# Two engines share the making of sample-wise mixing matrices, with a new order around samples 2, 3 and the last ones

## The reference

```python
# conv step: groups = 4, K = 9, pad = 4
out = conv(x, weight) + (c @ c_weight.T)[:, :, None] + bias[None, :, None]
x = x + out
# mix step
h = gelu(embedding @ W0 + b0); h = gelu(h @ W1 + b1)
att = softmax(h @ W2 + b2)                        # 64 x 8
agg_w = einsum('bk,koi->boi', att, weight)        # one 128x128 matrix per sample
agg_b = att @ bias_k
x = x + einsum('boi,bih->boh', agg_w, x) + agg_b[:, :, None]
```

## Time and profile before

| what | value |
|---|---|
| runs | median 726.98 us of 3, 726.56 to 728.69 |
| the profiled execution | 725.75 us, with a span of 723.6 us from its first to its last instruction |
| busy share of the span | PE 99%, PEld 86%, ACT 83%, POOL 76%, DVE 64% |
| granted TensorE clock | 0.999 of full speed |
| DMA | 177.56 MB, mean 245 GB/s |

### The profile page before, as it was taken

The page is one execution under the profiler, slowest core; times in us unless marked ns, Lnnn a source line. Parts: engine busy times, 40 slices in busy tenths (PEclk is TensorE's granted clock), DMA queues, the critical chain, the costliest instruction groups (busy, mean ns, idle before and its releaser), DMA issues.

```text
span 723.6 us, 29229 instructions
## 1 busy us (share of the span) xinstructions
PE 713.3 (99%) x12419; PEld 622.5 (86%) x12419; DVE 465.5 (64%) x413; ACT 598.6 (83%) x456; POOL 546.6 (76%) x592
## 2 busy tenths in 40 slices
PE   8999999999999999999999999999999999999996
PEld 6899998998888888888888888888888888888885
DVE  6987667577777666566566566566566566576543
ACT  5988887888888888888888888888888888888843
POOL 2899999999999999866766766766766766767740
PEclk9999999999999999999999999999999999999999
DMA  6445867867876867887787778678768777777546
GB/s 225 158 151 183 285 229 241 286 201 268 283 248 230 293 237 254 281 271 255 249 291 258 241 262 287 225 250 275 268 225 294 245 249 269 243 249 270 191 156 239
DMA packets 66551, 177.56 MB, mean 245 GB/s; under 512 B 7437, under 2 KB 50008, under 8 KB 50264
## 3 DMA queue, kind: packets, MB, share of 16 engines
q1 hardware_dynamic: 66002, 176.93, 71.4%
q10 hardware_dynamic: 518, 0.17, 0.1%
HBM read 101.57 MB, written 75.50 MB: 245 GB/s over the span
## 4 chain that ended last, share of the span: by engine, by line
PE 82%; POOL 11%; DMA 4%; issue 1%; SPq 1%; DVE 0%; ACT 0%; DVEq 0%; POOLq 0%; ACTq 0%
PE ps L432 61%; PE ps L463 21%; POOL mix_prod L755 4%; POOL mix_prod L750 4%; DMA mix_dram<-mix_parts 2%; POOL mix_sum_f L758 2%; DMA mix_rep<-mix_dram 1%; DMA x_in<-in_x_dram 1%; POOL mix_f L762 1%; SPq L291 1%; POOL mix_parts L768 1%; POOL mix_parts L765 0%; ACT x_hi L515 0%; POOL par L745 0%; POOL par L774 0%
## 5 line engine op out<-in xcount | busy, mean ns | idle before, releaser
L432 PE MATMUL ps<-x_hi,cw_hi 32*128 32x512 f32 x3072 | 384.8, 385 | 0.9 <-ACT x_hi L515 0.6
L432 PE MATMUL ps<-x_hi,cw_lo 32*128 32x512 f32 x3072 | 384.1, 384 | 0.0
L511 ACT ACTIVATE x_ph<-x_in 128x2560 f32<-128x2560 f32 x63 | 318.6, 5058 | 2.7 <-DMA x_in<-in_x_dram 2.1
L613 DVE TENSOR_TENSOR y_lo<-ps,y_hi 128x512 fp32r<-128x512 f32 x256 | 159.2, 684 | 239.1 <-ACT y_hi L524 239.1
L432 PE MATMUL ps<-x_lo,cw_hi 32*128 32x512 f32 x3072 | 274.7, 385 | 0.0
L432 PEld LDWEIGHTS ps<-x_lo,cw_hi 32*128 32x128 f32 x3072 | 222.1, 183 | 21.1 <-issue 0.8
L463 PE MATMUL ps<-y_hi,mix_rep 32*128 32x512 f32 x2048 | 214.4, 385 | 1.6 <-DMA mix_rep<-mix_dram 1.6
L432 PEld LDWEIGHTS ps<-x_hi,cw_hi 32*128 32x128 f32 x3072 | 195.3, 183 | 22.6 <-issue 1.7
L432 PEld LDWEIGHTS ps<-x_hi,cw_lo 32*128 32x128 f32 x3072 | 194.8, 183 | 20.3 <-issue 0.2
L537 ACT ACTIVATE z_out<-ps,par 128x1024 f32<-128x1024 f32 x124 | 146.1, 1236 | 75.3 <-PE ps L463 75.3
L602 DVE TENSOR_TENSOR x_lo<-x_ph,x_hi 128x2560 fp32r<-128x2560 f32 x63 | 189.4, 3007 | 2.2
(11 more groups left out here) (80 smaller groups left out, 92.7 us busy)
## 6 DMA issues: line engine op xcount, KB each, us to landing
x_in<-in_x_dram SPq DMA_DIRECT2D x64, 1024.0 KB, 7.3
out_dram<-z_out SPq DMA_DIRECT2D x63, 1024.0 KB, 5.0
mix_rep<-mix_dram SPq DMA_DIRECT2D x256, 128.0 KB, 2.6
mix_dram<-mix_parts SPq DMA_DIRECT2D x64, 128.0 KB, 7.0
out_dram<-x_in SPq DMA_DIRECT2D x2, 512.0 KB, 3.5
z_out<-in_L_cond_weight_dram SPq DMA_DIRECT2D x1, 512.0 KB, 3.9
cw_nat<-in_L_cond_weight_dram SPq DMA_DIRECT2D x1, 144.0 KB, 2.2
w_sb<-in_L_cond_W_dram ACTq DMA_DIRECT2D x2, 64.0 KB, 5.1
```

The lines of the kernel that those rows point to most:

```text
L432: mm = pe.matmul(y_at(s)[:, g, :], w[rows, m, :], x_at(xx[buf(s)], rows, m), start=i == 0, stop=i == CONV - 1)
L511: nc.scalar.activation(x_ph[buf(s)][:, :, :, :], by_lane(x_in[buf(s)]), ACT.Copy).then_inc(x_split_ph, 1)
L613: nc.vector.tensor_tensor(y_lo[s[1]][:, g, :], y_at(s)[:, g, :], y_hi[s[1]][:, g, :].bitcast(F32), ALU.subtract).then_inc(y_lo_made, 1)
```

## The change

GpSimd makes the matrices of the first three samples (`FIRST = 3`) with the same instructions as before, outside any loop. VectorE makes all others, at the end of its slot: a copy of the weights, eight terms that are summed in two chains (`mix_even`, `mix_odd`; the identity is added with the first odd term), and three instructions for the two halves. In the slot before the last, VectorE makes two matrices, those of samples 62 and 63.

In slot 2, VectorE takes y(2)'s rests ahead of x(3)'s. SP's order differs in the last slots. In DRAM a matrix lies as 32 rows of 4 KB (a row holds the four groups' two halves) where it lay as 128 rows of 1 KB.

```diff
+FIRST = 3
...
-        mix_dram = [nc.dram_tensor(f"mix_dram{k}", [P, 2, P], F32, kind="Internal").ap() for k in range(2)]
+        mix_dram = [nc.dram_tensor(f"mix_dram{k}", [Q, G, 2, P], F32, kind="Internal").ap() for k in range(2)]
...
+        def by_pool(s):
+
+            return isinstance(s[0], int) and number(s) < FIRST
...
-                sp.dma_start(mix_dram[b][:, :, :], mix_parts[b][:, :, :].bitcast(F32)).then_inc(mix_stored[b], DMA)
+                sp.dma_start(mix_dram[b].rearrange("c g h o -> g c (h o)"),
+                             mix_parts[b].rearrange("p h o -> p (h o)").bitcast(F32)).then_inc(mix_stored[b], DMA)
...
-                    sp.dma_start(rep_at(s)[Q * r:Q * r + Q, :, :, :].bitcast(F32).rearrange("c g h o -> c g (h o)"),
-                                 mix_dram[b].rearrange("(g c) h o -> c g (h o)", g=G)).then_inc(mix_loaded[b], DMA)
+                    sp.dma_start(rep_at(s)[Q * r:Q * r + Q, :, :, :].bitcast(F32).rearrange("c g h o -> c (g h o)"),
+                                 mix_dram[b].rearrange("c g h o -> c (g h o)")).then_inc(mix_loaded[b], DMA)
...
             def slot(s):
-                load_mix(after(s, -1))
+                if is_sample(s, NS - 1):
+                    store_mix(s)
+                    load_mix(after(s, -1))
+                    load_mix(s)
+                    return
+
+                if not is_sample(s, NS):
+                    load_mix(after(s, -1))
                 store(after(s, -3))
+                if is_sample(s, NS - 2):
+                    store(after(s, -2))
                 load(after(s, AHEAD))
                 store_mix(s)
...
+            def mix_matrix(s):
+
+                if not exists(s) or by_pool(s):
+                    return
+
+                at_least(dve, z_read, done(s, 2, lag=-U))
+                if is_sample(s, FIRST):
+                    dve.wait_ge(par_made, FIRST)
+                a = par[s[1]]
+                nc.vector.tensor_copy(a[:, :], table[:, number(s), :]).then_inc(par_made, 1)
+                dve.wait_ge(par_made, done(s))
+
+                for k in range(NK):
+                    part = (mix_even, mix_odd)[k % 2]
+                    if k == 0:
+                        nc.vector.tensor_scalar(part[:, :], mixw_t[:, k, :], a[:, k:k + 1], None,
+                                                ALU.mult).then_inc(mix_term, 1)
+                        continue
+                    if k >= 2:
+                        dve.wait_ge(mix_term, done(s, NK, lag=-FIRST - 1) + k - 1)
+                    nc.vector.scalar_tensor_tensor(part[:, :], mixw_t[:, k, :], a[:, k:k + 1],
+                                                   ident[:, :] if k == 1 else part[:, :],
+                                                   ALU.mult, ALU.add).then_inc(mix_term, 1)
+                dve.wait_ge(mix_term, done(s, NK, lag=-FIRST))
+                nc.vector.tensor_tensor(mix_f[:, :], mix_even[:, :], mix_odd[:, :], ALU.add).then_inc(mix_sum, 1)
+
+                at_least(dve, mix_stored[buf(s)], DMA * uses(s))
+                nc.vector.tensor_tensor(mix_parts[buf(s)][:, 0, :], mix_even[:, :], mix_odd[:, :],
+                                        ALU.add).then_inc(mix_sum, 1)
+                dve.wait_ge(mix_sum, done(s, 2, lag=-FIRST))
+                nc.vector.tensor_tensor(mix_parts[buf(s)][:, 1, :], mix_f[:, :],
+                                        mix_parts[buf(s)][:, 0, :].bitcast(F32),
+                                        ALU.subtract).then_inc(mix_made, 1)
+                dve.wait_ge(mix_made, done(s, lag=-FIRST))
+
             def slot(s):
                 if not is_sample(s, 0):
                     round_x(after(s, 1))
+
+                if not is_sample(s, 0) and not is_sample(s, 2):
                     rest_x(after(s, 1))
                 for g in range(G):
                     rest_y(s, g)
+                if is_sample(s, 2):
+                    rest_x(after(s, 1))
+                if not is_sample(s, NS - 1):
+                    mix_matrix(s)
+                if is_sample(s, NS - 2):
+                    mix_matrix(after(s, 1))
...
-            pipeline(pool, mix_matrix)
+            for b in range(FIRST):
+                mix_matrix((b // U, b % U))
```

More of the change, by code:

```diff
@@ L116, in cond_resid_kernel @@
         mix_sum_f = sb("mix_sum_f", [P, P])
+        mix_f_first = sb("mix_f_first", [P, P])
+        mix_even = sb("mix_even", [P, P])
+        mix_odd = sb("mix_odd", [P, P])
         mix_f = sb("mix_f", [P, P])
@@ L205, in cond_resid_kernel @@
         prod_made = sem("prod_made")
+        tree_sum = sem("tree_sum")
+        mix_hi_made = sem("mix_hi_made")
+        mix_first_made = sem("mix_first_made")
+        mix_term = sem("mix_term")
         mix_sum = sem("mix_sum")
-        mix_hi_made = sem("mix_hi_made")
         mix_made = sem("mix_made")
@@ L273, in store_mix @@
                 b = buf(s)
-                made, taken = ahead(done(s), DMA * G * uses(s))
-                sp.wait_ge(mix_made, made)
+                made, taken = ahead(done(s) if by_pool(s) else done(s, lag=-FIRST), DMA * G * uses(s))
+                if by_pool(s):
+                    sp.wait_ge(mix_first_made, made)
+                else:
+                    sp.wait_ge(mix_made, made)
                 at_least(sp, mix_loaded[b], taken)
-                sp.dma_start(mix_dram[b][:, :, :], mix_parts[b][:, :, :].bitcast(F32)).then_inc(mix_stored[b], DMA)
+                sp.dma_start(mix_dram[b].rearrange("c g h o -> g c (h o)"),
+                             mix_parts[b].rearrange("p h o -> p (h o)").bitcast(F32)).then_inc(mix_stored[b], DMA)
             def load_mix(s):
@@ L735, in mix_matrix @@
             def mix_matrix(s):
-                if not exists(s):
-                    return
                 at_least(pool, z_read, done(s, 2, lag=-U))
@@ L755, in mix_matrix @@
                     nc.gpsimd.tensor_tensor(mix_prod[:, 0:half, :], mix_prod[:, 0:half, :],
-                                            mix_prod[:, half:2 * half, :], ALU.add).then_inc(mix_sum, 1)
-                    pool.wait_ge(mix_sum, done(s, 3, lag=-1) + n + 1)
+                                            mix_prod[:, half:2 * half, :], ALU.add).then_inc(tree_sum, 1)
+                    pool.wait_ge(tree_sum, done(s, 3, lag=-1) + n + 1)
                 nc.gpsimd.tensor_tensor(mix_sum_f[:, :], mix_prod[:, 0, :], mix_prod[:, 1, :],
-                                        ALU.add).then_inc(mix_sum, 1)
-                pool.wait_ge(mix_sum, done(s, 3))
-                nc.gpsimd.tensor_tensor(mix_f[:, :], mix_sum_f[:, :], ident[:, :], ALU.add)
+                                        ALU.add).then_inc(tree_sum, 1)
+                pool.wait_ge(tree_sum, done(s, 3))
+                nc.gpsimd.tensor_tensor(mix_f_first[:, :], mix_sum_f[:, :], ident[:, :], ALU.add)
                 at_least(pool, mix_stored[buf(s)], DMA * uses(s))
@@ L767, in mix_matrix @@
                 pool.wait_ge(mix_hi_made, done(s))
-                nc.gpsimd.tensor_tensor(mix_parts[buf(s)][:, 1, :], mix_f[:, :],
+                nc.gpsimd.tensor_tensor(mix_parts[buf(s)][:, 1, :], mix_f_first[:, :],
                                         mix_parts[buf(s)][:, 0, :].bitcast(F32),
-                                        ALU.subtract).then_inc(mix_made, 1)
-                pool.wait_ge(mix_made, done(s))
+                                        ALU.subtract).then_inc(mix_first_made, 1)
+                pool.wait_ge(mix_first_made, done(s))
                 if is_sample(s, 0):
```

## The result

The changed kernel takes **757.23 us** (median of 6 runs, 755.55 to 760.0) where the kernel before takes 726.6 beside it: a ratio of 1.042 with an interval of 1.040 to 1.0445. It is 30.6 us slower; I had forecast 724.4. The profiled execution has 755.64 us, with a span of 753.8.

The account below looks back on a forecast made before the run. TensorE was taken as the bound, 10.88 us a sample. 3.17 us recovered less 0.1 and 0.8 at the end gives 2.3 less: 723.45 from the profiled execution, 724.7 from the median; forecast 724.4, range 723.2 to 727.2.

Parts of the forecast that it names:

- Cover 1.8 us with all at their worst: Steady stretch: VectorE's matrix lands by 716.8 with longest store and load, its mix due at 718.6.
- the four engines: Rival: the new layout's matrix store uses four of sixteen DMA engines, ending 1.17 us later, at 725.6; chance 0.22.
- That is hidden in the steady stretch (1.8), not at the end: Claim that a four-engine matrix store, 1.56 instead of 0.39 us, costs time only at the end, 1.17 us.
- 3.5 us a matrix: VectorE's twelve instructions per matrix take 3.5 us (bounds 2.5 and 4.8); up to 4.0 fit in a sample.
- the 0.36: Time in us of one VectorE tensor_tensor of 128, at 1.02 ns an element, used for the matrix's upper bound.
- y(2)'s rests: Slot 2 on VectorE: taken first, they end near 43.7, x(3)'s run to 47.0, and 0.70 us goes.
- the 0.70: Excess us between the mixes of samples 0 and 1, put down to late VectorE rests, not a late matrix.
- The early loss of 3.17 us: Excess over 10.88 us a sample, samples 0 to 61, mostly from GpSimd's late matrices; expected to go, less 0.1.
- The end, 1.0 us late: Matrix 62, behind out store 60 in SP's queue, reaches its mix 1.0 us late; the end loses 0.8.
- upper bound of 3.2: Largest lateness of matrix 62 at the end: ready at 713.6, its mix due at 710.46.
- lower bound of 709.9: Earliest arrival of matrix 62 at the end, with an empty queue and 2.13 us: late by nothing.
- I take nothing: Matrix loads from 4 KB DRAM rows, a quarter of the packets: no gain counted, at most help at the end.

Follow-up runs that it names:

- experiment 6: Changed kernel with the x load sent behind the matrix store from sample 3 on, four-engine store kept: 727.55 us, ratio 1.0014.
- experiment 10: Changed kernel with the old DRAM layout and the x load behind the matrix store from sample 3 on: 723.48 us, ratio 0.9957.
- experiment 3: Kernel before with only the store's destination split into 4 x 32 rows of 1 KB by spare rows: 768.09 us, ratio 1.054.
- experiment 5: Changed kernel with the out store behind the matrix store, except in sample 62's slot; four-engine store kept: 729.92 us, ratio 1.0035.
- experiment 7: Kernel before with only y(2)'s rests moved ahead of x(3)'s: 727.35 us, ratio 0.9996.
- experiment 1: Changed kernel with the matrix in DRAM as 128 rows of 1 KB again, store and loads as before: 728.09 us, ratio 1.0015.
- experiment 8: Changed kernel with the old DRAM layout and SP's old order in the last slots: 731.78 us, ratio 1.0057.
- experiment 9: Changed kernel with old layout, SP's old order at the end, and x load behind the matrix store from sample 3: 728.12 us, ratio 1.0003.
- experiment 11: Changed kernel with old layout, x load behind matrix store from sample 3, out store 60 behind matrix 62's store: 722.97 us, ratio 0.9954.
- experiment 4: Changed kernel with the matrix store split into four DMAs of 32 x 256, 4 KB rows kept: 733.97 us, ratio 1.011.

## Why the prediction was wrong, step by step

- **The step that failed** is "Cover 1.8 us with all at their worst", and from it, of the four engines, "That is hidden in the steady stretch (1.8), not at the end". That counted one matrix's way from VectorE to TensorE, once. What sets the pace is SP's round: store, landing, four loads, out store, x load, and only then the next store. A cover for one matrix says nothing of a round that repeats. A landing of 7.78 and the 3.2 us of SP's other issues make 11.0, already over 10.88. I read 7.78 as a delay of GpSimd's matrices.
- **The rival was the right mechanism.** Four engines was priced at 1.17 us more a store. Measured, it is 2.1 with little ahead in the queue (medians of 3.86 in experiment 6 and 1.72 in experiment 10, which differ in the layout alone) and 0.65 a round behind 2 MB (11.35 against the 10.70 of before). It stood in one place, the end, and it belongs in all 61 samples: 10.70 + 0.65 - 10.88 = 0.47 each, 29 us. With the rival's own 1.17 in the round, the loss would have come out at 60 us: the size was off by a factor of two, and it was counted once instead of 61 times. Experiment 3 shows that the store's shape is enough, experiments 5 and 6 that nearly all of the cost comes by way of SP's round; 4.1 us of it stay with the x load behind (experiment 6 against 10).
- **Feedback that I had not seen.** A late SP finds the matrix made, so it sends out store, x load and matrix store together, and the store is slow because of that. With 16 engines SP still comes back, at 10.70 a round in the stretch shown; with four it does not, at 11.35.
- **VectorE: 3.5 us a matrix**, measured 3.2, with 4.0 to be had: right, and it never was the bound. The terms came 0.26 us apart, as taken from the z copies. The row at 308.06, an fp32 tensor_tensor of 128, agrees at 0.29 with the figure that the prediction worked out from the Trainium skill ("VectorE: DVE Perf Modes", The TRN2 errata); the 0.36 that I had from longer rows was too much.
- **y(2)'s rests**: forecast from 41.6, and x(3)'s to end at 47.0; they start at 41.14, and x(3)'s run from 43.54 to 47.16 (3.62 us). Right in the mechanism. The argument that the 0.70 were no late matrix was loose, since its 52.4 lies behind 51.65, when mix 1 was due; experiment 7, where the 0.70 go, bears it out, and shows that alone this is worth nothing measurable.
- **The early loss of 3.17 us** was put down to GpSimd's pace, "an addition that takes 0.46 us alone took 2.92 us". That was a part at most: without GpSimd's matrices some of it stays (1.5 us in the trace of experiment 1, 7.6 in that of experiment 8, which differs only in SP's last slots), with the x load behind the store it goes (experiment 9). The two traces also show that 3.17, read from one execution, was no steady price.
- **The end, 1.0 us late**: 3.19 in the changed kernel itself, at the prediction's upper bound of 3.2, with the four-engine stores; 1.60 in experiment 1, 1.47 in experiment 10 with the old layout. Right in kind and too small; the cause is in part the second matrix that SP, by the change's own order, stores before it loads matrix 62 (the chain of experiment 11). The lower bound of 709.9 had left that out.
- **4 KB rows, "I take nothing"** holds for the loads (a median of 2.7 us to landing, 2.6 before); their price is in the store that they force.

The forecast's 724.4 is near the 723.5 of experiment 10, but that is luck: experiment 10 has the old layout and another order of SP, and neither stood in the forecast.

## What to carry to other kernels

Sum up the round of each in-order queue, with the landing that it waits for inside, against the time of one iteration, before you call anything on it hidden; the waits of that queue tell whether it has any slack. A small transfer that others wait for goes ahead of the large ones in its queue, not behind them. When a layout changes, look at how the first dimension of both sides of each DMA changes, not at its row size alone.

## What the hardware showed that I had not expected

- A store of 128 KB takes 1.72 us from its issue to its loads with little ahead of it in the queue (experiment 10, median of 51), and right behind two transfers of 1 MB a median of 7.16 (kernel before, 50 stores; late in the run SP's waits for TensorE are in it too). Its place in the queue weighs far more than its number of engines (3.86 with four, experiment 6).
- The same bytes to the same rows of 1 KB, in 4 x 32 rows with a gap between instead of 128 without, cost 41 us of 727 (experiment 3).
- Splitting the store into four DMAs regains the engines, but SP is busy issuing for 3.38 us instead of 0.75 (experiment 4).
